# Second attention: the row maxima are split by GpSimd before a bf16 transpose, and ScalarE copies the shift rows out

## The reference

```python
q = (x_norm @ w_q)...        # 16 heads of 8
k = (x_norm @ w_k)...        # 4 heads of 8
q, k = q * rf, k * rf
qkt = jnp.einsum('brkqa,bkca->brkqc', q5, k) / scale
attn = jax.nn.softmax(qkt, axis=-1)
s = jnp.einsum('brkqc,bkca->brkqa', attn, v)
o = s @ w_o
return s + o
```

## Time and profile before

| | |
|---|---|
| median of 3 runs | 1651.19 us (1650.28 to 1651.6) |
| span of the profiled execution | 1651.9 us |
| TensorE busy | 1455.9 us (88%) |
| VectorE busy | 1180.7 us (71%) |
| ScalarE busy | 946.4 us (57%) |
| GpSimd busy | 833.9 us (50%) |

### The profile page before, as it was taken

The page is one execution under the profiler, slowest core; times in us unless marked ns, Lnnn a source line. Parts: engine busy times, 40 slices in busy tenths (PEclk is TensorE's granted clock), DMA queues, the critical chain, the costliest instruction groups (busy, mean ns, idle before and its releaser), DMA issues. The chain is left out here.

```text
span 1651.9 us, 30013 instructions
## 1 busy us (share of the span) xinstructions
PE 1455.9 (88%) x9488; PEld 716.9 (43%) x9488; DVE 1180.7 (71%) x3123; ACT 946.4 (57%) x1805; POOL 833.9 (50%) x941
## 2 busy tenths in 40 slices
PE   3999999969993279999999999999999999849996
PEld 1444444469993123333333333333333332239996
DVE  3688777833334568899889998899989998514443
ACT  2565556524441147777777778777777777612221
POOL 4688888743003463556555655556565620114443
PEclk9999999979997569999999999999999999969998
DMA  1111211289995111122112221122212210347771
GB/s 38 46 56 54 64 56 49 80 242 298 304 296 145 57 56 46 56 77 73 55 55 65 78 61 54 57 75 73 59 55 62 70 51 13 108 155 239 236 241 58
DMA packets 144965, 165.76 MB, mean 100 GB/s; under 512 B 29073, under 2 KB 115217, under 8 KB 142649
## 3 DMA queue, kind: packets, MB, share of 16 engines
q1 hardware_dynamic: 92377, 74.76, 15.2%
q10 hardware_dynamic: 38608, 58.62, 11.6%
q0 software_dynamic: 13824, 30.47, 6.0%
HBM read 111.93 MB, written 51.30 MB: 99 GB/s over the span
## 5 line engine op out<-in xcount | busy, mean ns | idle before, releaser
L1592 DVE TENSOR_REDUCE c_mx<-c_ps_mx 128x1 f32<-128x512 f32 x1024 | 649.8, 683 | 89.6 <-PE c_ps_mx L1828 82.1
L1496 ACT ACTIVATE c_pt<-c_ps_e 128x512 f32<-128x512 f32 x1024 | 567.1, 601 | 189.9 <-PE c_ps_e L1798 176.3
L1798 PE MATMUL c_ps_e<-c_qst,c_kex 74*128 74x512 bf16 (+1 forms) x1024 | 347.7, 388 | 3.5 <-ACT c_pt L1496 1.9
L1811 PE MATMUL c_ps_v<-c_pt,c_vp 128*32 128x512 f32 x2048 | 274.5, 608 | 1.1 <-ACT c_pt L1496 0.7
L1333 POOL DMA_INDIRECT c_gy<-ys,mt x128 | 124.2, 970 | 276.5 <-PE c_ps_v L1811 129.9
L1828 PE MATMUL c_ps_mx<-c_kex,c_qst 64*128 64x512 bf16 x1024 | 204.6, 396 | 57.9 <-DVE c_mx L1592 40.9
L1828 PEld LDWEIGHTS c_ps_mx<-c_kex,c_qst 64*128 64x128 bf16 x1024 | 49.3, 93 | 367.8 <-DVE c_mx L1592 345.3
L998 PE MATMUL f_ps_h<-f_xT,f_w 128*128 128x256 f32 x800 | 197.0, 386 | 0.2 <-DVE f_xT L1064 0.2
L558 ACT ACTIVATE a_pt<-a_ps_s,temp 128x1024 f32<-128x1024 f32 (+3 forms) x128 | 113.1, 884 | 91.3 <-PE a_ps_s L652 86.3
L499 POOL DMA_INDIRECT xs<-a_xn,a_meta x128 | 135.6, 1059 | 38.1 <-issue 35.3
L998 PEld LDWEIGHTS f_ps_h<-f_xT,f_w 128*128 128x128 f32 x800 | 145.4, 194 | 15.9 <-issue 0.6
(11 more groups left out here) (225 smaller groups left out, 1895.0 us busy)
## 6 DMA issues: line engine op xcount, KB each, us to landing
f_w<-in_we ACTq DMA_DIRECT2D x80, 321.0 KB, 4.4
f_w<-in_we ACTq DMA_DIRECT2D x37, 576.0 KB, 4.5
c_qst<-qparts SPq DMA_DIRECT2D x75, 192.0 KB
f_x<-rows SPq DMA_DIRECT2D x40, 257.0 KB, 3.9
f_x<-xs SPq DMA_DIRECT2D x80, 128.0 KB, 4.4
ys<-f_y ACTq DMA_DIRECT2D x80, 128.0 KB, 4.3
qparts<-c_qp SPq DMA_DIRECT2D x16, 384.0 KB, 2.5
x<-in_x SPq DMA_DIRECT2D x16, 256.0 KB, 3.0
```

The source lines that it names most:

```text
L1496: nc.scalar.activation(pt[:, s % 4, hl, :], ps_e[:, e_bank(64 * b + n)], ACT.Exp, scale=QSCALE).then_inc(exp_done, 1)
L1592: nc.vector.tensor_reduce(mx[:, g % 2, col:col + 1], ps_mx[:, m_bank(64 * b + 2 * m + par)], AX, ALU.max).then_inc(mx_done, 1)
L1798: nc.tensor.matmul(ps_e[:, e_bank(64 * b + n)], kex[rows, p, k_head(hl), kt * P:(kt + 1) * P], qst[rows, p, q_head(g, hl), :], start=True, ...
L1811: last = nc.tensor.matmul(ps_v[32 * hl:32 * (hl + 1), :], vp[:, p, kt, hl, :], pt[:, s % 4, hl, :], start=kt == 0, stop=kt == NT - 1)
```

## The change

- `mx` shrinks from 128 columns per buffer to the 16 that are used.
- GpSimd gets `split`: it rounds the group's maxima to bf16 (high part) and subtracts this from the maxima (low part), both into a new tile `mxp` (128 partitions x 2 buffers x 2 parts x 16). It waits for the group's last row maximum and for the transpose that read the buffer.
- TensorE transposes the 32 bf16 columns in a matmul against a bf16 identity. It waits for `split` instead of for VectorE.
- ScalarE copies the 32x128 result out with a scale of -1 (`shifts`, behind the first exponential of steps 1, 5, 9 and 13); VectorE's two operations are gone.
- VectorE begins a new group in a buffer when `split` has read it, no more when the transpose has.
- SyncE's DMAs read the new layout; their number and size are the same.

In GpSimd's body the four splits stand at its very start (group 1), between the norms and `normal_rows` (group 2), behind the four scatters (group 3), and ahead of `k_parts` (the next batch's group 0).

```diff
@@ -1156,8 +1156,9 @@
         qst = sb("c_qst", [P, 2, H1, L], BF16)
         kex = sb("c_kex", [P, 2, KV1, L], BF16)
         ones2 = sb("c_ones2", [2, KV1 * L], BF16)
-        mx = sb("c_mx", [P, 2, P])
-        shb = sb("c_shb", [NT * HL, 2, 2, P], BF16)
+        mx = sb("c_mx", [P, 2, NT * HL])
+        mxp = sb("c_mxp", [P, 2, 2, NT * HL], BF16)
+        shb = sb("c_shb", [2 * NT * HL, 2, P], BF16)
         pt = sb("c_pt", [P, 4, HL, L])
         ov = sb("c_ov", [P, L])
         rcp = sb("c_rcp", [P, NT, HL])
@@ -1197,8 +1198,8 @@
          oh_ready, rank_ps, rank_used, slot_ready, const_in) = sems(
             "mx_ps", "mx_done", "mt_ps", "sh_r", "s_ps", "exp", "pv", "ov_sb", "ot_ps", "ot_sb", "sT_ps", "sT_sb",
             "wo_ps", "wo_sb", "oh_r", "rank_ps", "rank_u", "slot_r", "const")
-        dve_pro, dve_ln, dve_sh, dve_ot, row_steps, part_steps, made, vp_made, next_tokens, kept_xn, q_half = sems(
-            "dve_pro", "dve_ln", "dve_sh", "dve_ot", "row_steps", "part_steps", "made", "vp_made", "next_tokens", "kept_xn", "q_half")
+        dve_pro, dve_ln, split_steps, split_ready, dve_ot, row_steps, part_steps, made, vp_made, next_tokens, kept_xn, q_half = sems(
+            "dve_pro", "dve_ln", "split_steps", "split_r", "dve_ot", "row_steps", "part_steps", "made", "vp_made", "next_tokens", "kept_xn", "q_half")
 
         with nc.Block() as block:
 
@@ -1277,7 +1278,7 @@
                         for n in range(2):
                             row = SHIFT_ROW[par] + n
                             sp.dma_start(qst[row:row + 1, p, first:first + 2, :],
-                                         shb[8 * par:8 * par + 8, g % 2, n, :]).then_inc(sh_in[g % 2], 16)
+                                         shb[16 * n + 8 * par:16 * n + 8 * par + 8, g % 2, :]).then_inc(sh_in[g % 2], 16)
 
                 def body(i, o):
                     prev, nxt, nxt2, nxt3 = flags(i, o)
@@ -1427,11 +1428,22 @@
                         rows2_d, bass.IndirectOffsetOnAxis(ap=bsl[:, p, t:t + 1], axis=0),
                         row[:, p, t, :], None).then_inc(scattered[p], 16)
 
+                def split(i, o, g):
+
+                    b, h, p = batch(i, o)
+                    pool.wait_ge(mx_done, 16 * (4 * b + g + 1) + 2)
+                    if not (isinstance(b, int) and 4 * b + g < 2):
+                        pool.wait_ge(mt_ps, 4 * b + g - 1)
+                    nc.gpsimd.tensor_copy(mxp[:, g % 2, 0], mx[:, g % 2]).then_inc(split_steps, 1)
+                    pool.wait_ge(split_steps, 4 * b + g + 1)
+                    nc.gpsimd.tensor_tensor(mxp[:, g % 2, 1], mx[:, g % 2], mxp[:, g % 2, 0], ALU.subtract).then_inc(split_ready, 1)
+
                 ln = Chain(pool, row_steps, LN_POOL_C, k.passed_pool)
                 pc = Chain(pool, part_steps, PART_POOL_C, k.passed_pool)
 
                 def body(i, o):
                     prev, nxt, nxt2, nxt3 = flags(i, o)
+                    split(i, o, 1)
                     if nxt2:
                         combine(ln, i, o + 2)
                     if nxt:
@@ -1439,10 +1451,13 @@
                     keep_xn(i, o)
                     if nxt2:
                         norms(ln, i, o + 2)
+                    split(i, o, 2)
+                    if nxt2:
                         normal_rows(i, o + 2)
                     if prev:
                         for t in range(NT):
                             scatter(i, o - 1, t, 5 + t)
+                    split(i, o, 3)
                     if nxt3:
                         gather(i, o + 3, (0,), 9)
                     if nxt2:
@@ -1450,6 +1465,8 @@
                     if nxt3:
                         gather(i, o + 3, (1,), 11)
                         gather(i, o + 3, (2,), 12)
+                    if nxt:
+                        split(i, o + 1, 0)
                     if nxt2:
                         k_parts(pc, i, o + 2)
                     if nxt3:
@@ -1474,6 +1491,7 @@
                 combine(ln, 0, 1)
                 norms(ln, 0, 1)
                 normal_rows(0, 1)
+                split(0, 0, 0)
                 pool.wait_ge(const_in, 48)
                 rotate(0, 1)
                 gather(0, 2, range(2 * NT))
@@ -1501,6 +1519,13 @@
                     act.wait_ge(ot_ps, 4 * b + g)
                     nc.scalar.activation(ov[:], ps_v[:], ACT.Copy).then_inc(ov_sb, 1)
 
+                def shifts(i, o, g):
+                    b, h, p = batch(i, o)
+                    act.wait_ge(mt_ps, 4 * b + g + 1)
+                    if not (isinstance(b, int) and 4 * b + g < 2):
+                        act.wait_ge(sh_in[g % 2], 64 * (2 * b + g // 2))
+                    nc.scalar.activation(shb[:, g % 2, :], ps_j[0:2 * NT * HL, 0:P], ACT.Copy, scale=-1.0).then_inc(sh_ready, 1)
+
                 def xT_copy(i, o):
                     b, h, p = batch(i, o)
                     act.wait_ge(xT_ps, b + 1)
@@ -1549,6 +1574,10 @@
                     prev, nxt, nxt2, nxt3 = flags(i, o)
                     for s in range(16):
                         exps(i, o, s, 0)
+                        if s in (1, 5, 9):
+                            shifts(i, o, s // 4 + 1)
+                        if s == 13 and nxt:
+                            shifts(i, o + 1, 0)
                         if s == 7 and nxt2:
                             xT_copy(i, o + 2)
                         for hl in range(1, HL):
@@ -1570,6 +1599,8 @@
 
                 for o in range(2):
                     xT_copy(0, o)
+                    if o == 1:
+                        shifts(0, 0, 0)
                     prj_copy(0, o, 0)
                     prj_copy(0, o, 1)
                     kT_copy(0, o)
@@ -1585,23 +1616,12 @@
                     b, h, p = batch(i, o)
                     g = m // 8
                     if m % 8 == 0 and not (isinstance(b, int) and 4 * b + g < 2):
-                        dve.wait_ge(mt_ps, 4 * b + g - 1)
+                        dve.wait_ge(split_ready, 4 * b + g - 1)
                     dve.wait_ge(mx_ps, 32 * b + m + 1)
                     for par in range(2):
                         col = 8 * par + m % 8
                         nc.vector.tensor_reduce(mx[:, g % 2, col:col + 1], ps_mx[:, m_bank(64 * b + 2 * m + par)], AX,
                                                 ALU.max).then_inc(mx_done, 1)
-
-                def shifts(i, o, g):
-                    b, h, p = batch(i, o)
-                    dve.wait_ge(mt_ps, 4 * b + g + 1)
-                    if not (isinstance(b, int) and 4 * b + g < 2):
-                        dve.wait_ge(sh_in[g % 2], 64 * (2 * b + g // 2))
-                    src = ps_j[0:NT * HL, 0:P]
-                    nc.vector.tensor_scalar(shb[:, g % 2, 0, :], src, -1.0, None, ALU.mult).then_inc(dve_sh, 1)
-                    dve.wait_ge(dve_sh, 4 * b + g + 1)
-                    nc.vector.scalar_tensor_tensor(shb[:, g % 2, 1, :], src, -1.0, shb[:, g % 2, 0, :],
-                                                   ALU.mult, ALU.subtract).then_inc(sh_ready, 1)
 
                 def normalise(i, o, g):
                     b, h, p = batch(i, o)
@@ -1700,16 +1720,12 @@
                             row_max(i, oo, 2 * m)
                         if s == 0 and nxt:
                             choose(i, o + 1)
-                        if s in (1, 5, 9):
-                            shifts(i, o, s // 4 + 1)
                         if s == 2 and nxt:
                             choose_index(i, o + 1)
                         if s == 3 and nxt:
                             one_hot(i, o + 1)
                         if s == 12 and nxt:
                             keep_x1(i, o + 1)
-                        if s == 13 and nxt:
-                            shifts(i, o + 1, 0)
                         if more:
                             row_max(i, oo, 2 * m + 1)
                         if s == 1 and prev:
@@ -1778,8 +1794,6 @@
                 for m in range(AHEAD):
                     for j in range(2):
                         row_max(0, 0, 2 * m + j)
-                    if m == 3:
-                        shifts(0, 0, 0)
                 bodies(dve, body)
                 normalise(0, NB - 1, 3)
                 output(0, NB - 1)
@@ -1889,8 +1903,9 @@
                 def max_columns(free, i, o, g):
                     b, h, p = batch(i, o)
                     pe.wait_ge(*free)
-                    pe.wait_ge(mx_done, 16 * (4 * b + g + 1) + 2)
-                    nc.tensor.transpose(ps_j[:, 0:P], mx[:, g % 2, :], k.ident[:]).then_inc(mt_ps, 1)
+                    pe.wait_ge(split_ready, 4 * b + g + 1)
+                    nc.tensor.matmul(ps_j[0:2 * NT * HL, 0:P], mxp[:, g % 2].rearrange("p n c -> p (n c)"), k.ident_b[:],
+                                     start=True, stop=True).then_inc(mt_ps, 1)
                     return sh_ready, 4 * b + g + 1
 
                 def token_rows(free, i, o, g):
```

## The result

The changed kernel takes 1775.47 us (median of 4 runs, 1774.49 to 1781.17) against 1650.94 us before: 1.0759 times as long, 95% interval 1.0739 to 1.0778. Forecast were 1744 us and a range of 1712 to 1785. The direction, the mechanism and its four places were right; one term of the sum, the clock's, was much too small.

A forecast was written before the change was run, and what follows sets the result against it. VectorE sets the pace from step 15 to 6 of a body, TensorE's own order from 6 to 14. The span of 1651.9 us plus 84 for stops and 9 for clock falls led to 1744 us, range 1712 to 1785.

The forecast's parts named there:

- The four places and the stops: At steps 0, 4, 8, 12 of a body (one batch of 16 steps), TensorE's small transpose waits for GpSimd's late split.
- The stops without the clock: Second attention: net cost of TensorE's waits for splits, without falls of its granted clock, 84 us in sum.
- step-4 stop: Split behind the norms at step 4 of a body: TensorE stops 2.2 us, net 2.1, 14 times.
- The split's own length: GpSimd's two operations with the hand-over to TensorE take 0.65 us per split, bounds 0.6 and 0.8.
- The clock: TensorE's granted clock falls after every second stop of step 4: 7 x 1.3 = 9 us; bounds none and 71.
- Rival 2: TensorE's clock falls at most stops, three to four a body, 52 to 71 us: 1787 to 1806 us; chance 0.13.
- The range: Whole kernel, 1712 to 1785 us; the upper end has 25 of 55 stops with a fall and splits of 0.8 us.
- The relief of VectorE: Losing its two shift operations, 0.64 us per group, counts at steps 1 and 5 of a body: at most 20 us.
- rival 3: Transpose waits are covered and VectorE's relief at steps 1 and 5 wins, 18 to 20 us: 1631 to 1633; chance 0.05.
- bodies 14 and 15: The last two batches have a free GpSimd at step 0 and gain 0.64 us each: -1.3 us.
- ScalarE's copies at nothing: 64 copies of 32x128 behind the first exponential of steps 1, 5, 9, 13 cost nothing; 19 us if uncovered.
- The first body: Body 0's split behind eight gathers stops TensorE 7.7 us; two later waits shrink, net +3.6 us, bounds 0 and 8.

The follow-up runs named there:

- Dead splits: Kernel before, with the 64 splits added on GpSimd at the changed kernel's places but read by nobody: 1654.40 us, ratio 1.0008.
- the fill: Changed kernel, with seven needless bf16 matmuls ahead of each small transpose that has to wait, to keep TensorE busy: 1728.66 us, ratio 1.0459.
- three matmuls: Changed kernel, with three instead of seven needless matmuls ahead of each small transpose that has to wait: 1732.53 us, ratio 1.0475.
- the relief run: Kernel before, without VectorE's two shift operations and nothing on GpSimd; ScalarE makes one copy, the low part left at zero: 1653.52 us, ratio 1.0001.

## Why the prediction was right, and where its sum was off

- *The four places and the stops.* Right. GpSimd's strict order put the split behind something at each of the 55 forecast places, TensorE waited 1.3 to 1.9 us (2.34 at step 4 of the first body), and where a split is moved its stop goes. Dead splits cost nothing. The stops without the clock cost 77 us (the fill), forecast were 84; a full body 5.24 us against 1.2 + 2.1 + 1.3 + 1.3 = 5.9. The step-4 stop was 1.93 us instead of 2.2. The fill measures the stops fairly: with three matmuls a body is as long as with seven.
- *The split's own length.* 0.64 us measured, 0.65 forecast from rows for other sizes: right as a sum. Of its terms no run shows the 0.07 us for the hand-over to TensorE; it was my estimate. From the recorded end of the second operation at step 0, 968.95 + 0.22 = 969.17, to the transpose at 969.31 are 0.14 us, and the two operations are shorter than the 0.24 us taken for each, 0.20 and 0.22.
- *The clock.* The term that was mis-sized: 9 us forecast, 46.8 measured. Both factors were low. I took a fall for every second stop of step 4, 7 in all; there are 28 of 3.4 us and the long one, all but one behind stops of step 4 and step 8. And no run shows the forecast's 1.3 us a fall: with two falls a body is 61.45 - 58.05 = 3.4 us longer, 1.7 us a fall, half of the 3.4 us that it lasts. The 1.3 came from two steps that are not alike, 617.06 - 611.99 = 5.07 us at the clock 0.50 and 938.54 - 935.38 = 3.16 us at 1.00, as 3.4 x (1 - 3.16/5.07): the high one holds four transposes of the output, the low one only the small transpose.

```profile
616.85 0.42 PE L1893 MATMUL c_ps_j<-ident,c_mx 128*128 128x128 f32 x1
...
937.79 0.60 PE L1840 MATMUL c_ps_j<-ident,c_ov 128*128 128x128 f32 x4
938.23 0.38 PE L1798 MATMUL c_ps_e<-c_qst,c_kex 74*128 74x512 bf16 x1
```

  The four take 938.23 - 937.79 = 0.44 us of the 3.16. The instructions of the low step take 2.83 us together at the high clock, which makes 3.4 x (1 - 2.83/5.07) = 1.5 us; what makes up the rest to 1.7 stays open. Of the two rows that I weighed against each other, the one that spoke for many falls (2.63 of 4 us busy, then low) pointed the right way here, though a stop with 2.41 of 4 us busy stayed high. Rival 2 had three or four falls a body, two were measured; 1775 lies nearer to its 1787 than to the forecast of 1744.
  Of the 54 stops of 1.3 to 1.9 us in the changed kernel 28 had a fall behind them, and none had when they were filled. The waits of 0.16 to 0.56 us that the kernel before has in front of its three banks of maxima, 29.1 us in 104 waits and 0.74 us at the longest, had none: its clock stays at 1.00 from 640 to 1440 us.
- *The range.* That the time fell inside 1712 to 1785 is in part luck. The upper end allowed for 25 falls at 1.3 us, 33 us, and the falls cost 46.8. What made room for the other 14 us were the 8 us set aside for splits of 0.8 us, which measured 0.64, and stops that cost 7 us less than forecast.
- *The relief of VectorE.* The bound of 20 us for it was wrong, and with it rival 3: there was nothing to be had. I had read "VectorE runs without a gap" as "VectorE sets the pace". At step 1 the next row maximum depends on a pair of matmuls that TensorE issued without waiting (923.38); that row was in the trace of the kernel before. In the sum only the 1.3 us for bodies 14 and 15 rested on it, so it didn't show.
- *ScalarE's copies at nothing.* Nothing measured speaks against it: they take 0.25 us each, and the relief run, which has 64 of them, of 0.25 us too, is as fast as the kernel before.
- *The first body.* 3.6 us forecast, 5 by the timed runs, 5.2 to 5.5 by the trace. The stop of step 4 goes with that of step 0, 2.34 us that the sum had entered under step 4.
- *Rival 4*, TensorE catching up by half, is out: of the 97.7 us that the small transposes wait, 77 stay in the end time without the clock.

Left open: which of a body's stops the clock falls behind. It was step 4 and step 8 here, with the stop of step 12 as long as that of step 8 and no fall; with step 4's stop away it fell behind step 12 in half of the bodies. No run held the stops and shifted them against each other.

## What to carry to other kernels

When work is handed to an engine that looks half idle, look up what stands directly ahead of each handed-over instruction in that engine's order, and when that ends against the moment at which the result is asked for; the busy share says nothing about it (GpSimd was 49% busy here and TensorE waited 97.7 us for it). Before an engine without gaps is relieved, look at the instruction behind the one to be removed: if its input was issued without a wait for this engine, the time removed becomes a hole (0.56 us at step 1 here). And price short stops of TensorE twice, once as the stops and once as falls of the clock behind them: 77 and 46.8 us here.
